# Padded rows of a DRAM scratch copy, and a prologue in another order, in a fused attention and expert kernel

## The reference

```python
# layer 1: causal attention, 16 heads of 8
scores = einsum('bhqd,bhkd->bhqk', Q, K) / sqrt(8)       # Q, K, V = projections of layernorm(x)
attn = einsum('bhqk,bhkv->bhqv', softmax(where(causal, scores, -inf)), V)
y = einsum('bhsv,hdv->bsd', attn, WO)
# layer 2: every row goes to one of 8 experts, the one with the largest x @ centroids.T
h = relu(layernorm(xs, ln_g[e], ln_b[e]) @ w1[e].T + b1[e])
ye = xs + h @ w2[e].T + b2[e]
out = alpha * ye + (1 - alpha) * xs                      # alpha = sigmoid(largest affinity)
```

## Time and profile before

| | us |
|---|---|
| median of 3 runs | 404.59 |
| lowest, highest | 403.49, 404.85 |
| the profiled execution | 405.06 |
| its span in the profile | 403.3 |

### The profile page before, as it was taken

One profiled execution on the slowest core, in us unless ns is written; L12 is line 12 of the kernel. 1 busy time (PEld: TensorE's weight loads), 2 busy tenths in 40 slices (PEclk: granted clock), 3 DMA queues, 4 the chain that ended last, 5 costly groups with the idle time before them and its releaser, 6 DMA issues.

```text
span 403.3 us, 10952 instructions
## 1 busy us (share of the span) xinstructions
PE 316.1 (78%) x3517; PEld 252.9 (63%) x3548; DVE 333.7 (83%) x1253; ACT 234.9 (58%) x574; POOL 239.9 (59%) x321
## 2 busy tenths in 40 slices
PE   2447879989999998999989988987105999998940
PEld 1325657766776776776667766754105999997930
DVE  7956798989899999799889988888661999998970
ACT  2201675675685685675765865556105898886940
POOL 4741373664675675665764765648540388887782
PEclk9998999999999999999999999999656999999995
DMA  7663674745735636636546546012035667666600
GB/s 209 117 115 36 114 167 62 124 109 66 133 75 78 113 79 81 110 66 93 97 78 89 99 82 107 25 35 68 21 95 172 183 190 195 181 190 174 182 31 6
DMA packets 34823, 42.82 MB, mean 106 GB/s; under 512 B 5481, under 2 KB 25197, under 8 KB 33232
## 3 DMA queue, kind: packets, MB, share of 16 engines
q1 hardware_dynamic: 31888, 37.49, 46.7%
q0 software_dynamic: 2304, 4.37, 3.4%
q10 hardware_dynamic: 576, 0.27, 0.3%
HBM read 30.65 MB, written 11.66 MB: 105 GB/s over the span
## 4 chain that ended last, share of the span: by engine, by line
PE 35%; POOL 20%; DMA 15%; DVE 13%; issue 12%; ACT 2%; SPq 1%; POOLq 1%; DVEq 0%; ACTq 0%
DMA aug<-nmT 11%; POOL out_x L546 9%; PE O L868 5%; POOL rsz L556 5%; PE S L834 5%; DVE nmf L1107 4%; PE ST L847 4%; PE S L829 3%; PE S L827 3%; PE MB L794 2%; PE O L872 2%; POOL xs_rows L479 2%; DMA aug<-qk_parts 2%; PE MB L882 2%; PE ST L856 2%
## 5 line engine op out<-in xcount | busy, mean ns | idle before, releaser
L1107 DVE TENSOR_REDUCE nmf<-S 128x2 f32<-128x512 f32 (+1 forms) x192 | 130.5, 683 | 25.0 <-PE S L834 14.2
L620 ACT ACTIVATE p<-ST 128x1024 f32<-128x1024 f32 x64 | 65.5, 1023 | 29.4 <-PE ST L847 29.2
L459 POOL TENSOR_SCALAR_AFFINE_SELECT p<-p 128x512 f32<-128x512 f32 x64 | 40.9, 639 | 51.4 <-ACT p L624 51.1
L455 POOL TENSOR_SCALAR_AFFINE_SELECT p<-p 128x512 f32<-128x512 f32 x64 | 40.8, 638 | 26.8 <-ACT p L620 26.4
L834 PE MATMUL S<-aug 126*128 126x128 bf16 x512 | 50.7, 222 | 0.0
L546 POOL DMA_INDIRECT out_x<-vaug,x_all x39 | 42.0, 1078 | 7.9 <-issue 7.9
L847 PE MATMUL ST<-aug 128*128 128x256 bf16 x256 | 38.6, 272 | 7.5 <-DMA aug<-nmT 6.6
L868 PE MATMUL O<-p,vaug 128*32 128x256 f32 x512 | 41.1, 390 | 2.5 <-POOL p L455 2.5
L834 PEld LDWEIGHTS S<-aug 126*128 126x128 bf16 x512 | 40.4, 99 | 3.5
L829 PE MATMUL S<-causal,identb 128*128 128x256 bf16 x128 | 36.0, 281 | 7.5 <-issue 4.5
L479 POOL DMA_INDIRECT xs_rows<-x_all,pos x32 | 32.8, 1026 | 10.9 <-issue 6.3
(11 more groups left out here) (162 smaller groups left out, 824.1 us busy)
## 6 DMA issues: line engine op xcount, KB each, us to landing
w1s<-in_w1x SPq DMA_DIRECT2D x39, 259.0 KB
qk_parts<-qkp SPq DMA_DIRECT2D x16, 384.0 KB, 2.8
aug<-qk_parts SPq DMA_DIRECT2D x32, 192.0 KB
aug<-qk_parts SPq DMA_DIRECT2D x32, 128.0 KB
x_all<-xs_rows SPq DMA_DIRECT2D x39, 67.0 KB
aug<-qk_parts SPq DMA_DIRECT2D x32, 64.0 KB
w_tab<-in_w2t SPq DMA_DIRECT2D x8, 256.0 KB
out_x<-vaug,x_all POOLq DMA_INDIRECT x39
```

Of the source, the lines that this page charges most:

```text
L455: g.affine_select(out=v, in_=v, compare_op=ALU.is_ge, fill=0.0, base=0, pattern=[[0, 4], [1, P]], channel_multiplier=-1).then_inc(s["sel0" ...
L459: g.affine_select(out=v, in_=v, compare_op=ALU.is_ge, fill=0.0, base=0, pattern=[[0, 4], [1, P]], channel_multiplier=-1).then_inc(s["sel1" ...
L620: a.activation(p0[:, gr % 2], ST0[:, :, :], ACT.Exp, scale=SCALE).then_inc(s["exp0"], 1)
L1107: v.tensor_reduce(dst, S[:, n % 2].rearrange("p (j n) -> p j n", j=k), op=ALU.max, axis=AX_X, negate=True).then_inc(s["red"], 1)
```

## The change

Four edits. (1) In DRAM every row of `qk_parts` has 384 elements in place of 256, of which 256 are used. (2) POOL's fill of `kaug[0]` moves ahead of `power_x(0)`, that of `kaug[2]` behind `low(1)`; SP waits for buffers 0 and 1 before `parts_in(1)`, and for buffer 2 in step 0. (3) The memsets of `vaug[1]` and `vaug[2]` and their ones go from DVE to POOL, behind the scatter of the blank rows and ahead of `power_x(2)`, which moves behind them. (4) The six bn_stats of group 2 go between the first six maxima of batch 0, and `x_variance(2)` behind the first `shift_parts`.

```diff
-    qk_dram = nc.dram_tensor("qk_parts", (RING, 2, 3, DH, NH, SEQ), BF16, kind="Internal").ap()
+    qk_dram = nc.dram_tensor("qk_parts", (RING, 2, 3, DH, NH, SEQ + P), BF16, kind="Internal").ap()[:, :, :, :, :, 0:SEQ]
...
             parts_out(Nth(1))
-            sp.wait_ge(s["qzero"], 3)
-            sp.wait_ge(s["kone"], 3)
+            sp.wait_ge(s["qzero"], 2)
+            sp.wait_ge(s["kone"], 2)
             parts_in(Nth(1))
...
                     shift(b, 1)
+                if i.k == 0:
+                    sp.wait_ge(s["qzero"], 3)
+                    sp.wait_ge(s["kone"], 3)
                 if b := at(i, 2):
                     parts_in(b)
...
+            g.memset(kaug[:, 0].bitcast(F32), two_ones).then_inc(s["kone"], 1)
             pool.wait_ge(s["consts"], 2)
             power_x(0)
             power_x(1)
-            g.memset(kaug[:, 0].bitcast(F32), two_ones).then_inc(s["kone"], 1)
...
             g.memset(kaug[:, 1].bitcast(F32), two_ones).then_inc(s["kone"], 1)
+            low(Nth(1))
             g.memset(kaug[:, 2].bitcast(F32), two_ones).then_inc(s["kone"], 1)
-            low(Nth(1))
-            power_x(2)
-
...
                                  in_=fill[:, :], in_offset=None).then_inc(s["blank"], 16)
+            for p in (1, 2):
+                g.memset(vaug[:, p], 0.0).then_inc(s["vmem"], 1)
+            pool.wait_ge(s["vmem"], 2)
+            for p in (1, 2):
+                g.memset(vgroups(p)[:, :, 0, :, DH:DH + 1], 1.0)
+                g.memset(vgroups(p)[:, :, 1, :, 16 + DH:17 + DH], 1.0).then_inc(s["vones"], 1)
+            power_x(2)
             low(Nth(2))
...
-                    act.wait_ge(s["vones"], p + 1)
+                    act.wait_ge(s["vones" if p else "vone0"], max(p, 1))
...
             dve.wait_ge(s["x_rest"], 16)
-            x_stats(2)
-            x_variance(2)
-            v.memset(vaug[:, 1], 0.0)
-            v.memset(vaug[:, 2], 0.0).then_inc(s["vmem"], 1)
-            dve.wait_ge(s["vmem"], 2)
-            ones_of_values(1)
-            ones_of_values(2)
             for gr in range(NG):
                 for u in range(3):
                     maxima(Nth(0), gr, u)
+                    if gr < 2:
+                        x_stats(2, 3 * gr + u)
                 if gr % 2:
                     shift_parts(Nth(0), gr // 2)
+                if gr == 1:
+                    x_variance(2)
                 if gr == 2:
                     residue(Nth(2))
```

More of the change, by code:

```diff
@@ L208, in sandwich_kernel @@
         MB = ps("MB", [P, 512])
-        names = ("w_attn w_cent w_ffn x_in x_next x_rest qzero kone ids_r consts pmem vmem vones "
+        names = ("w_attn w_cent w_ffn x_in x_next x_rest qzero kone ids_r consts pmem vzero vone0 vmem vones "
                  "st_x agg_x ve_x rs_x nb_x xn_r xnT_r xnT_d qk_r hi_d r1_d mid_d parts_d "
@@ L1042, in ones_of_values @@
                 v.memset(vgroups(p)[:, :, 0, :, DH:DH + 1], 1.0)
-                v.memset(vgroups(p)[:, :, 1, :, 16 + DH:17 + DH], 1.0).then_inc(s["vones"], 1)
+                v.memset(vgroups(p)[:, :, 1, :, 16 + DH:17 + DH], 1.0).then_inc(s["vone0"], 1)
             def x_stats(n, k=None):
@@ L1282, in _ @@
             x_variance(1)
-            v.memset(vaug[:, 0], 0.0).then_inc(s["vmem"], 1)
-            dve.wait_ge(s["vmem"], 1)
+            v.memset(vaug[:, 0], 0.0).then_inc(s["vzero"], 1)
+            dve.wait_ge(s["vzero"], 1)
             ones_of_values(0)
```

## The result

The kernel after the change took 412.52 us in the median of six runs (409.0 to 416.52), the one before 404.72 (six runs, 402.76 to 407.5). The ratio is 1.0161, 95% interval 1.0115 to 1.0206: rival C's side. The profiled execution of the kernel after is the longest of its six, in a slower state that some executions of either kernel show and the ratios leave out, so its span of 414.7 us overstates the loss.

The account below looks back on a forecast made before the run. PE and DVE set the loop's pace, with parts_in nearly on the path through nmT. Terms: -0.4 (earlier key ones) + 0.74 (statistics between maxima) + 0 (padding) = +0.3 us, on a median of 404.59: 404.9 us, range 395 to 413.

Parts of the forecast that it names:

- rival C: parts_in slower from 16 times the runs, on the path at nmT and prologue; 10% gives 417, 5% 411; chance 0.28.
- A: Padding of the DRAM rows leaves the parts_in loads unchanged: 404.9 us, own range 403.5 to 407; chance 0.42.
- What differs is the destination: parts_in's slow long runs were put down to few destination partitions; these stay, so no change in load time.
- 0.85 us x 15 = 12.8: Price of parts_in loads 10% slower: 0.85 us each in the prologue and some 14 batches.
- close to its full amount in each: Loop: nmT waits behind parts_in with hardly slack, so longer loads cost nearly all their added time every batch.
- SP's own cost: SP's time to issue parts_in loads: 0.38 us for short or long runs, counted as nothing.
- against 8.66 now: Time taken for batch 0's parts_in before the change, from 17.30 to its last piece landing at 25.96.
- The lower bound: parts_in at 28 ns a run, perfectly spread: 2.7 us, so up to 6.0 us less.
- port estimate: From SBUF ports reached by the destination partitions: six loads of 1.2 us, together 7.2 us, however long the runs.
- The upper one: parts_in: 28 ns a short run on top of 59 ns for its 512 B, 1.5 times as long; called far off.
- real case: parts_in loads 10% longer, taken as the realistic slow outcome.
- B: parts_in faster because 8 KB runs at 8 KB pitch hindered one another: 394 (5 us less) or 399 (1 us); chance 0.30.

Follow-up runs that it names:

- e1: Only the DRAM rows padded to 384 elements, against the kernel before: 413.12 us, ratio 1.0169.
- e4: Kernel before with rows of 256 and every parts_in load split in two by heads: 400.33 us, ratio 0.9859.
- e2: Only the prologue's edits, rows of 256 as in the kernel before: 406.73 us, ratio 0.9983.
- e10: Rows of 384, with the nmT transfers issued by ACT on its own queue, ratio against the kernel before: 424.07 us, 1.0383.
- e11: Kernel before (rows of 256) with the nmT transfers issued by ACT on its own queue: 465.94 us, ratio 1.1369.
- e3: Kernel before with the keys' heads 272 elements apart in SBUF, so key loads move 512 B runs, DRAM unchanged: 406.3 us, ratio 1.0027.
- e5: Kernel before with DRAM rows padded to 512 elements, 256 used (512 B runs at 1024 B pitch): 408.91 us, ratio 1.0100.

## Why the prediction was right or wrong

- The range (395 to 413) held the time with half a microsecond to spare, and slower was forecast at 0.37, no more than faster; the likeliest case, A, was wrong. The step that failed is "What differs is the destination [...] That stays, so my central value for parts_in is no change". With the same partitions, bytes and DMAs, the padded rows alone cost 1.7%: 386 engine-us more in the queue, and nmT 1.22 us later in the mean of a batch.
- The mechanism of C was right, the loads on the path at nmT and in the prologue. It was priced at "0.85 us x 15 = 12.8" for 10% (with 404.9 that is 418, not 417), and 411 for 5%. Batch 0's loads took 11.33 us from first issue to the first scores in e1 against 10.70, 6% more. In the loop, nmT came 1.22 us later in 9.76, 12% more. At "close to its full amount in each" that would be some 18 us; the loop took 5.9 more. The time is near C's 5% by luck: the lateness was underrated, and how much of it lands on the path overrated.
- "SP's own cost: [...] I count nothing" was wrong in its size, 0.6 to 1.0 us a load in place of 0.3 to 0.4, and nearly right in what it is worth: SP takes 4.48 us to issue a batch's loads in place of 2.46 (means of 14), its pause takes up most of that, so that nmT is issued 0.41 us later, and e4 spends more on issues and is faster.
- The term "against 8.66 now" took a part for the whole: the row is the last load alone, from its issue at 17.30. From the first issue at 15.31 to 25.96 the six loads take 10.65 us. The lower bound, and the closeness to the 7.2 us of the port estimate, rest on that reading.
- The lower bound (the load 6.0 us shorter) was far off. The upper one (28 ns a run on top of 59, 1.5 times) was the nearer: q1's 386 engine-us more are 16 ns for each of 24,576 runs on top of the 59, 1.27 times in the engines' time. By the packets of the traces the loads took 1488 engine-us before and 1865 in e1, 1.25 times. The "real case" of 10% was too low for the engines' time.
- B did not come about: neither pitch tried, 768 or 1024 B, made anything faster. Both cut the runs to 512 B, so whether 8 KB runs at an 8 KB pitch hinder one another stays untested. The port estimate of the Trainium skill ("SBUF — State Buffer", "Door 1: The DMA port swizzle"), by which run length would not matter, isn't what these runs show: e1 was slower and e4 faster over the same partitions. Nor did padding by 4 KiB, reported to help in the Trainium skill's "DMA: Bandwidth & Descriptors", "Latency and other measured facts", at pitches far above this one, bring anything at 8 KB: e1, whose runs it also cut, was 1.7% slower.
- The prologue: 0.4 us gained up to the first load, as summed (0.40); in e2 the first scores came 0.65 sooner. The statistics cost 0.49, not 0.74: a maximum and its statistics together took 0.81 us in e2 (26.50 to 27.31), not the 0.67 + 0.21 of the sum. Missed was the slower stretch of PE behind shift_parts, about 0.5 us. The sum of +0.3 came out at +0.36 by the first ST matmuls of e2.
- "longer costs close to its full amount in each" did not hold: 1.22 us later costs 0.39 a batch, with the dip of the clock in it. The prediction read "hardly slack" from one batch (6.26 us); by the packets nmT's last run ended 3.29 to 6.98 us after its issue in the kernel before, so other batches had room.

Shown: the padding is the whole loss; with it the queue's work, nmT's arrival, PE's waits for it and the loop grow together, in five kernels. That nmT is late because of the loads ahead of it is read from the queue's order and from these arrivals; the runs that were to cut the link (e10, e11) didn't. Not shown: how much of the padding's cost is the length of the runs and how much the pitch, why short runs in all six loads cost six times what they cost in three, why splitting loads shortens them, and why two tensors in DRAM do.

## What to carry to other kernels

A small transfer that is waited for, issued behind a bulk load on the same queue, makes the bulk load's time part of the path, whatever the engines' shares say: look for it in the waits first, then at the bulk. Don't break one 8 KB run per partition into 512 B runs for a layout's sake, and try such a load in two pieces: it was worth 1.4% here, more than any edit of the diff. A queue of its own does not put a small transfer ahead: here it cost the second halves the place they had in front of the loads. And ask how late the awaited transfer comes in each batch, not only whether it is waited for: here the loop paid a third of the delay.

## What the runs showed of the hardware that I had not expected

- SP's time to issue a load depends on its shape: 0.34 and 0.37 us in the median (queries, keys) for one run per partition before, 0.68 and 0.67 for sixteen on the DRAM side (e1), 0.67 for the keys' sixteen on the SBUF side (e3). It isn't the shape alone: e3's query loads, of one run as before, took 0.49, issued in turn with the keys'. Nor is it the number of runs alone: a parts_out of 768 runs took 0.38.
- Twelve loads of half the size kept q1 busy for 2807 engine-us, six for 3013.
- An 8 KB transfer in 32 runs landed 11.45 us after issue on a second queue (e11), against 7.93 at most on the chain behind the loads in the same queue.
- The pitch of the DRAM rows counts even at 512 B runs: 3399 engine-us in q1 at 768 B, 3262 at 1024 B (e1, e5).
